# First attention: VectorE computes each low part of the next projections ahead of that step's product of exponents and weights

## The reference, cut to what matters

```python
scores = jnp.einsum('bhqd,bhckd->bhcqk', q, kc) * scale
w = jax.nn.softmax(scores.astype(jnp.float32), axis=-1).astype(q.dtype)
chunk_out = jnp.einsum('bhcqk,bhckd->bhcqd', w, vc)
sum_w = w.sum(axis=-1, keepdims=True)
combined = (chunk_out * sum_w).sum(axis=2)
total = sum_w.sum(axis=2)
out = combined / (total + 1e-09)
```

## Time and profile before

| | |
|---|---|
| median of 3 runs | 2284.84 us (2283.74 to 2292.18) |
| profiled execution, its own time | 2275.93 us |
| its span | 2274.1 us |
| TensorE busy | 1991.5 us (88%) |
| VectorE busy | 1440.8 us (63%) |
| ScalarE busy | 970.6 us (43%) |
| first attention, batch 0 | from 33 us to about 556 us |
| first attention, batch 1 | from about 1153 us to about 1676 us |

### The profile page before, as it was taken

One profiled execution on the slowest core, in us unless ns is written; L12 is line 12 of the kernel. 1 busy time (PEld: TensorE's weight loads), 2 busy tenths in 40 slices (PEclk: granted clock), 3 DMA queues, 4 the chain that ended last, 5 costly groups with the idle time before them and its releaser, 6 DMA issues.

```text
span 2274.1 us, 31809 instructions
## 1 busy us (share of the span) xinstructions
PE 1991.5 (88%) x10080; PEld 1149.5 (51%) x10080; DVE 1440.8 (63%) x2432; ACT 970.6 (43%) x1358; POOL 572.6 (25%) x543
## 2 busy tenths in 40 slices
PE   5899999997897999997778999999969889999975
PEld 3444444443684555546544444444337655555554
DVE  5587777875527676852366777778662377676432
ACT  2444444441234566551224444444412246656411
POOL 0000000000000787884110000000000037797921
PEclk7899999999796999997959999999979979999977
DMA  2255555567200000000503665666670000000015
GB/s 91 55 142 143 142 145 140 147 154 194 99 1 10 1 10 6 1 1 29 163 29 85 147 150 144 148 151 151 157 231 1 1 10 10 1 6 1 1 60 148
DMA packets 84847, 187.99 MB, mean 83 GB/s; under 512 B 17698, under 2 KB 46755, under 8 KB 83107
## 3 DMA queue, kind: packets, MB, share of 16 engines
q1 hardware_dynamic: 83650, 183.76, 31.2%
q0 software_dynamic: 1024, 2.10, 0.3%
HBM read 178.47 MB, written 8.91 MB: 82 GB/s over the span
## 4 chain that ended last, share of the span: by engine, by line
PE 60%; DVE 18%; issue 10%; ACT 7%; DMA 2%; POOL 1%; SPq 1%; DVEq 0%; ACTq 0%; POOLq 0%
PE PS L792 7%; PE PS L762 5%; PE PS L747 4%; PE PS L752 3%; PE PS L902 3%; PE PS L730 3%; DVE mx L1834 3%; PE PS L962 3%; DVE EE L1863 3%; PE PS L942 3%; PE PS L1133 3%; PE PS L945 2%; PE PS L857 2%; ACT EE L1455 2%; DVE mrow L1967 2%
## 5 line engine op out<-in xcount | busy, mean ns | idle before, releaser
L1834 DVE TENSOR_REDUCE mx<-PS 128x8 f32<-128x512 f32 x512 | 330.8, 686 | 195.6 <-PE PS L730 191.0
L1455 ACT ACTIVATE EE<-PS 128x1024 f32<-128x1024 f32 x256 | 261.7, 1022 | 265.1 <-PE PS L752 264.3
L2333 POOL TENSOR_TENSOR Esum<-Esum,EE 128x512 f32<-128x512 f32 (+3 forms) x320 | 337.5, 1082 | 14.7 <-POOL Esum L2333 10.1
L1863 DVE TENSOR_TENSOR EE<-EE,V 128x1024 f32<-128x1024 f32 x256 | 310.2, 1218 | 40.9 <-DMA V<-weight_rows 40.4
L792 PE MATMUL PS<-EE,Vlater 128*64 128x512 f32 x1024 | 275.3, 617 | 29.5 <-DVE EE L1863 28.9
L2287 POOL TENSOR_TENSOR U<-xn,norm_aff 128x1024 f32<-128x1024 f32 x2 | 4.7, 2356 | 1108.4 <-DVE QA L2258 1108.4
L1967 DVE TENSOR_REDUCE mrow<-PS 128x1 f32<-128x512 f32 (+3 forms) x384 | 202.6, 551 | 85.3 <-PE PS L905 66.1
L747 PE MATMUL PS<-QA,KA 128*128 128x512 f32 x512 | 201.5, 475 | 10.5 <-ACT EE L1455 9.3
L730 PE MATMUL PS<-KA,QA 128*128 128x512 f32 x512 | 183.1, 437 | 8.1 <-DVE KB L1818 3.4
L1538 ACT ACTIVATE EE<-PS 128x1024 f32<-128x1024 f32 (+2 forms) x192 | 137.7, 738 | 104.2 <-PE PS L945 102.0
L752 PE MATMUL PS<-QB,KB 80*128 80x512 f32 x512 | 165.2, 404 | 0.0
(11 more groups left out here) (306 smaller groups left out, 3320.9 us busy)
## 6 DMA issues: line engine op xcount, KB each, us to landing
V<-weight_rows SPq DMA_DIRECT2D x512, 256.0 KB, 4.4
EE<-in_w SPq DMA_DIRECT2D x48, 192.0 KB, 2.7
V<-in_Wg SPq DMA_DIRECT2D x4, 1024.0 KB, 6.1
EE<-in_Wu SPq DMA_DIRECT2D x4, 1024.0 KB, 11.6
EE<-in_Wd SPq DMA_DIRECT2D x4, 1024.0 KB, 13.6
sorted_out<-U SPq DMA_DIRECT2D x12, 256.0 KB, 3.2
wo<-in_wo SPq DMA_DIRECT2D x5, 512.0 KB, 3.7
wq_s<-in_wq SPq DMA_DIRECT2D x17, 128.0 KB, 2.8
```

What stands on the lines that cost most here:

```text
L1455: act.activation(EE[i % 2][:, t, :], banks(0), ACT.Exp, scale=QSCALE).then_inc(s["p2_exp"], 1)
L1834: dve.tensor_reduce(mx[:, t, half * 8:half * 8 + 8], banks(5 + x % 2, BANK).rearrange("p (c k) -> p c k", c=8), AX, ALU.max).then_inc(s["p ...
L1863: dve.tensor_tensor(EE[i % 2][:, t, :], EE[i % 2][:, t, :], weight_ring[a % 2][:, odd, :], ALU.mult).then_inc(p3_mul, 1)
L2333: ins = pool.tensor_tensor(Esum[:, h, lo:hi], Esum[:, h, lo:hi], e_tile(t)[:, h, lo - t * P:hi - t * P], ALU.add)
```

## The change

In VectorE's `head0` the call of `low_next` moves from the end of the step to the place right behind the step's maxima, ahead of `weigh`.

```diff
                     for t in range(NT):
                         if i + 1 < HEADS:
                             maxima(i + 1, UNITS0[t])
+                        if t in [4, 5, 6, 7]:
+                            low_next(i, *divmod([4, 5, 6, 7].index(t), 2))
                         if t >= LAG_WEIGH and i >= 1:
                             weigh(i - 1, t - LAG_WEIGH)
                         if t < LAG_WEIGH and i >= 2:
                             weigh(i - 2, t + NT - LAG_WEIGH)
...
                             if t == 5:
                                 ins.then_inc(se_norm, 1)
-                        if t in [4, 5, 6, 7]:
-                            low_next(i, *divmod([4, 5, 6, 7].index(t), 2))
                     if i + 2 < HEADS:
                         maxima(i + 2, UNITS_FIRST)
```

## The result

The changed kernel takes 2302.42 us (median of 6 runs, 2295.46 to 2310.97) against 2285.64 us (2283.74 to 2293.07); the ratio is 1.0065, with a 95% interval of 1.0043 to 1.0087. It is slower by 10 to 20 us, where 18.8 us were forecast. This ratio and those of the experiments are each against executions of the kernel before taken beside them. Two executions of the kernel before, taken beside the second set of e4 and beside e8, took 2405.37 and 2568.15 us at a lower mean granted clock (0.80 and 0.72) and are left out of these ratios.

A forecast was written before the change was run, and what follows sets the result against it. TensorE was taken to bound the kernel, working in order with little idle time. Losses of 9.40 us per batch, 18.8 us for both, on the median 2284.84 gave 2303.6 us; own range 2298 to 2311, wider range 2291 to 2316.

The forecast's parts named there:

- Step 7 brings nothing: Fourth low part, q heads: it waits for ScalarE's high part until 140.39 anyway, so putting it first gains nothing.
- Steps 4 and 5: q heads: the product ends 0.84 us later, so TensorE's value products start 0.58 and then 0.84 us late.
- Step 6, the inherited wait: q heads: tile 0's product falls behind the third low part's wait; TensorE starts at 141.24 instead of 138.77.
- The sum: Per batch 5 x 1.07 (q heads) + 2 x 1.29 (k heads 5, 9) + 0.74 (head 1) + 0.73 (head 12) = 9.40 us.
- ScalarE's chain: Step 5, q heads: ScalarE's copy waits for the late value product, making the third high part behind it 0.84 us late.
- The waits: Profile after: TensorE's wait for products grows some 35 us; VectorE's for high parts about 2 us per q head, 1 per k head.
- the first row: TensorE's wait for low parts ahead of the chunk sums: 20.4 us shrinks to head 0's and head 12's, about 4 to 5.
- An earlier bank 4: Rival, ahead of the chunk sums: bank 4 comes free earlier and their wait goes, at most 16.3 us faster, 2268.5 us; chance 0.04.
- the wait that is filled by itself: Rival, step 6: the third high part is ready when VectorE arrives, so only reordering counts; 11.1 us, 2295.9 us; chance 0.11.
- that nothing moves: Rival: VectorE's instructions are not late where it counts, and the time stays at 2285 us; chance 0.03.
- The clock: Rival: TensorE's clock falls behind some 1.6 us idle in changed q heads, at least 1.70 us more each; 2320.6 us; chance 0.12.

The follow-up runs named there:

- e4: Projections, high parts and low parts one step earlier, low parts still behind the products, against the kernel before: 2274.18 us, ratio 0.9952; second run 2271.69 us, 0.9933.
- e8: On e4, the product of tile 2 moved from step 0 to the end of step 7: 2250.01 us, ratio 0.9845 to the kernel before.
- e1: Low part ahead of the product in step 7 alone, against the kernel before: 431.04 and 431.00 us per batch, ratio 1.0012.
- e3: Low part ahead of the product in steps 4 and 5 only, against the kernel before: 436.81 and 436.87 us per batch, ratio 1.008.
- e2: Low part ahead of the product in steps 6 and 7 only, against the kernel before: 436.28 and 436.33 us per batch, ratio 1.0056.
- e7: e4's projections and high parts, with low parts ahead of the product in steps 3, 4, 6 and 7: 430.81 and 430.75 us per batch, ratio 0.9994.
- e5: The studied change on top of e4, low parts ahead of the product in steps 3 to 6: 2349.24 us, ratio 1.0265 to the kernel before.
- e6: The changed kernel with ScalarE's copy of the finished head moved from step 6 to the head's end: 2312.36 us, ratio 1.0105 to the kernel before.

## Why the prediction was right

The direction, the mechanism and the size were right. The forecast was 2303.6 us and the median is 2302.42; against the time before, 18.8 us were forecast on the median and the runs give 10 to 20. The attention itself lost 20.5 us. That the median came within 1.2 us is luck: the runs of one kernel spread over some 15 us, and the sum was 1.7 us too small for the attention, while the medians moved by 16.8 us.

*Step 7 brings nothing.* Shown by e1, to 0.01 us in heads 4 to 10.

*Steps 4 and 5.* TensorE was to be 0.58 and 0.84 late and was 0.58 and 0.85 late. e3 shows that this reaches the end of the head in full.

*Step 6, the inherited wait.* Shown by e2 and, in reverse, by e7; e5 shows what two of them do. But the term was too small, by 0.05 to 0.13 us per head. I took 0.05 to 0.06 us from the end of a product to TensorE's start. For tile 0 it is 141.49 - 141.35 = 0.14, while in steps 5 and 6 of the same head it is 0.05. Tile 0's value product has two further waits ahead of the one for the product (for the copied head and for the values); that these cost the extra time is my reading of the code and wasn't tried.

*The sum.* By heads, forecast and measured: q heads 1.07 and 1.20, heads 5 and 9 1.29 and 1.35, head 1 0.74 and 0.84, head 12 0.73 and 0.78. Per batch 9.40 and 10.2 to 10.3.

*ScalarE's chain.* I let the copy of the finished head carry the lateness to the third high part. e6 shows that the projection on TensorE carries it as well: without the copy the third high part comes only some 0.2 us earlier and the q heads gain 0.17 us. So this step of the prediction named one of two carriers; the size hardly depended on that.

*The waits.* The growth of TensorE's wait for products was 35.4 us, with some 35 forecast. In head 12 the chunk sums still start 0.05 us behind the end of the fourth low part, as forecast (0.69 us from 448.20 on, rows below). But this lies only 0.17 us behind the place that the value product allows, 1.01 us behind its start, and it isn't listed as a wait, so the first row came out at 4.1 us. VectorE's wait for the high parts grew by 21.9 us over 12 q heads, 1.8 each (2 forecast), and by 5.3 us over 6 k heads, 0.9 each (1 forecast).

```profile
447.76 1.08 PE L792 MATMUL PS<-EE,Vlater 128*64 128x512 f32 x4 [1.60 <-DVE EE L1863]
...
448.20 0.69 DVE L1811 TENSOR_TENSOR QA<-PS,QA 64x512 fp32r<-64x512 f32 x1
...
448.94 3.64 PE L762 MATMUL PS<-EE,consts 128*32 128x512 f32 x32
```

*The rivals.* An earlier bank 4 is refuted by e1, the wait that is filled by itself by the 2.25 us in the timeline, and that nothing moves by the 10.3 us per batch. The clock stayed: chunk sums took 3.64 us behind an idle time of 1.66 us. e5, where it fell in each q head, shows that this rival was a real one. The prediction's sign for it was head 0, where 2.07 us of idle time had gone with a fallen clock; e1 shows that this doesn't always happen (last section), so a comparison of idle times alone doesn't tell how near the change was.

## What to carry to other kernels

When an engine's instruction waits for another engine, what stands in front of it is free as far as it fits into the wait, and what stands behind it is late; before moving the waiting one forward, look up when its input is there. A wait that disappears from the list of waits may only have changed its name: compare the sum over all waits of the engine that binds. What shortened this kernel was to start the input earlier (e4) and to pull a needed product into a stretch in which its engine was idle (e8).

## What the runs showed of the hardware that was not expected

The granted clock of TensorE fell in every q head of e5, in heads 2, 6, 10 and 12 behind an idle time of 1.73 to 1.76 us, in heads 4 and 8 at or behind a second one of 2.3 us. 1.60 to 1.66 us in the changed kernel and 1.76 us in head 12 before left it at 1.00. In head 0 of the kernel before, 2.07 us went with a fallen clock in both batches. In e1 head 0 has the same instructions; in batch 0 its clock fell and its chunk sums took 5.34 us, but in batch 1 the clock stayed at 1.00 behind the same idle time:

```profile
1214.87 3.64 PE L762 MATMUL PS<-EE,consts 128*32 128x512 f32 x32 [2.07 <-DVE QA L1811]
```

So no single length of an idle time separates the two outcomes, and the same instructions behind the same idle time can have either. In e5 head 2 took 35.66 us in batch 0 at a mean granted clock of 0.90 and 34.28 us in batch 1 at 0.95. What decides it stays open.

From head 15 of batch 0 to head 0 of batch 1 the kernels here have the same code but for the two ends, and the profiled executions took 687.6 to 703.8 us for it. Those up to 690.2 us had a mean granted clock of 0.88 to 0.89 in it, those of 699.3 us and more 0.86 to 0.87. Here the kernel before and e2, which have the same code there (numbers as in the earlier trace rows):

```profile
521.87:1209.94 688.07, 581.78 (x3069) 376.82 (x3070) 389.19 (x707) 280.72 (x424) 285.95 (x269) 0.88 0.14 42
525.77:1229.54 703.77, 595.49 (x3069) 387.41 (x3070) 390.11 (x707) 280.93 (x423) 286.06 (x269) 0.86 0.14 41
```

The same 3069 matmuls kept TensorE busy for 13.7 us longer, of the 15.7 us between the two. This is enough to hide or to feign an effect of this size in the totals: by the stretches of the attention the change costs 0.90% (the totals say 0.65%), e3 0.45% (0.80%) and e6 0.77% (1.05%). The stretches of the profile told 10 us per batch to 0.1 us.
